# First dt transfers, sums and logarithms of the woven block moved ahead of the expert stage, and the last block's silus, convolutions and rows reordered

## What is computed

```
# first layer, attention place: a selective scan (8 groups of 128 inner features, 16 states)
hs, gate = in_proj(x)                      # 1024 + 1024
u   = silu(causal_conv4(hs) + cb)          # taps, then silu
ts, Bm, Cm = x_proj(u)                     # low rank 128, then 16 + 16 state rows
dt  = softplus(ts @ dt_proj + dt_b)
h_t = exp(dt_t * A) * h_(t-1) + (dt_t * u_t) * B_t
y   = (sum over states of h_t * C_t + D * u) * silu(gate);   out = y @ out_proj
# second layer: RWKV-like attention; a second selective scan on ctx (4 groups);
# a mixture of 8 experts (top 2 of a softmax router) and one shared expert: 33 tiles of 128 hidden features
out = sum_e C[t, e] * (silu(x @ Wg_e) * (x @ Wu_e)) @ Wd_e + sigmoid(x @ Wsg) * shared(x)
x = layernorm(x + out)
```

## Time and profile before

| | us |
|---|---|
| median of 3 runs (lowest, highest) | 4272.32 (4268.02, 4273.85) |
| profiled execution, its own time | 4263.87 |
| its span | 4262.0 |
| PE, DVE, ACT, POOL busy | 3528.0, 3220.0, 1624.2, 1278.1 |

### The profile page before, as it was taken

How to read it: one execution, slowest core, us unless ns; L and a number is a source line. 1 busy time by engine, 2 the same in 40 slices (tenths; PEclk the granted TensorE clock), 3 DMA queues, 4 the chain that set the end, 5 groups by cost and what they waited for, 6 DMA issues and landing times. The chain is left out here.

```text
span 4262.0 us, 40434 instructions
## 1 busy us (share of the span) xinstructions
PE 3528.0 (83%) x14823; PEld 1466.2 (34%) x14823; DVE 3220.0 (76%) x2759; ACT 1624.2 (38%) x2173; POOL 1278.1 (30%) x452
## 2 busy tenths in 40 slices
PE   5777759887899859887899859887899859875898
PEld 1222233333333333333333333333333333322443
DVE  5998469777899669778899668868899758866333
ACT  4766333124555233214655333213555343212101
POOL 1544204332344203342344303342244303332000
PEclk8888979989899979989899979989799979976999
DMA  4888402221233302122233302122233301110222
GB/s 156 306 324 315 160 15 82 70 82 65 89 99 102 126 16 74 67 81 75 81 99 102 133 16 74 67 77 79 72 103 104 121 32 67 67 60 15 87 92 77
DMA packets 91350, 418.52 MB, mean 98 GB/s; under 512 B 14224, under 2 KB 26640, under 8 KB 88720
## 3 DMA queue, kind: packets, MB, share of 16 engines
q1 hardware_dynamic: 69264, 384.44, 25.3%
q10 hardware_dynamic: 21888, 31.43, 2.8%
HBM read 320.45 MB, written 70.25 MB: 92 GB/s over the span
## 5 line engine op out<-in xcount | busy, mean ns | idle before, releaser
L276 PE MATMUL ps<-r,ring 128*128 128x512 bf16 (+2 forms) x2040 | 802.0, 394 | 0.0
L1105 POOL TENSOR_TENSOR hh<-hh,bc 128x2048 f32<-128x2048 f32 x72 | 337.8, 4692 | 1023.9 <-DVE hh L1028 1023.9
L273 PE MATMUL ps<-r,ring 128*128 128x512 bf16 (+2 forms) x1384 | 558.3, 404 | 95.1 <-POOL r L259 29.4
L273 PE MATMUL ps<-xr,ring 128*128 128x512 bf16 x1568 | 622.3, 397 | 12.7 <-DMA ring<-wsplit 12.7
L277 PE MATMUL ps<-xr,ring 128*128 128x512 bf16 x1568 | 619.4, 395 | 0.0
L277 PE MATMUL ps<-r,ring 128*128 128x512 bf16 (+2 forms) x1384 | 557.7, 404 | 0.0
L1105 POOL TENSOR_TENSOR bc<-bc 128x2048 f32<-128x2048 f32 x64 | 299.2, 4675 | 350.2 <-DVE bc L1028 350.2
L1105 POOL TENSOR_TENSOR r<-r,bc 128x2048 f32<-128x2048 f32 x56 | 262.7, 4691 | 314.3 <-DVE r L1028 314.3
L1028 DVE TENSOR_TENSOR_SCAN hh<-da,hh 128x2048 f32<-128x2048 f32 x72 | 328.0, 4555 | 13.0 <-ACT da L966 11.8
L1069 DVE TENSOR_TENSOR xc<-xc,ps 128x512 f32<-128x512 f32 x176 | 119.3, 678 | 249.5 <-PE ps L277 249.5
L1028 DVE TENSOR_TENSOR_SCAN bc<-da,bc 128x2048 f32<-128x2048 f32 x64 | 289.2, 4519 | 0.5
(11 more groups left out here) (244 smaller groups left out, 6507.3 us busy)
## 6 DMA issues: line engine op xcount, KB each, us to landing
ring<-wsplit SPq DMA_DIRECT2D x304, 768.0 KB, 4.2
r<-wstream SPq DMA_DIRECT2D x76, 768.0 KB, 7.4
wsplit<-ring SPq DMA_DIRECT2D x58, 768.0 KB, 4.7
da<-r ACTq DMA_DIRECT2D x384, 63.9 KB, 2.0
wsplit<-r SPq DMA_DIRECT2D x18, 768.0 KB, 6.1
r<-xT SPq DMA_DIRECT2D x7, 1024.0 KB, 5.5
r<-gates_dram SPq DMA_DIRECT2D x3, 2048.0 KB, 9.7
bc<-guwT SPq DMA_DIRECT2D x4, 1024.0 KB, 7.4
```

The costliest lines, as they stand in the source:

```text
L273: mm = pe.matmul(out, w_hi, x_hi, start=start, stop=False)
L276: pe.matmul(out, w_hi, x_lo, start=False, stop=False)
L1105: pool.tensor_tensor(quartet(s), quartet(s), k.out_rows, ALU.mult).then_inc(read, 1)
```

## The change

In `close_batch` the dt products get four banks and move ahead of the rows, ACT's and DVE's parts of them move with them, both logarithms stand where they were but fewer operations lie before and behind, only the first `total` stays, and the first dt*u group and the first two fetches of the expert stage are done here (one by SP, one by ACT, which also loads the exp table). In `hidden_and_scan` (expert stage) those are left out, the second half of the sum is done by DVE at step 1, and the early loads are issued by ACT at step 31 instead of by SP. In `second_preparation` (with a store) ACT takes all x copies, taps and the first silu before the norm's squares and the other silus before its factors; POOL makes three low halves of y0 before the first of the silus; three of the low-rank products move ahead of mix(3); the rows get four banks, and DVE copies the first four of them.

```diff
1077.84 1.40 DVE L368 ScanInputs: dt_bank(j) = self.dt_banks[j % len(self.dt_banks)], used by magnitude, positive and dt_product
-        if j >= 2:
-            pe.wait_ge(self.zread, j - 1)
+        if j >= len(self.dt_banks):
+            pe.wait_ge(self.zread, j - len(self.dt_banks) + 1)
1077.84 1.40 DVE L368 spread_row
-            if self.row_banks == self.banks:
-                pe.wait_ge(self.zread, self.J)
+        if r < count:
+            taken = [j + 1 for j in range(self.J) if self.dt_banks[j % len(self.dt_banks)] == self.row_banks[r]]
+            if taken:
+                pe.wait_ge(self.zread, taken[-1])
1077.84 1.40 DVE L368 second_preparation, tensor
+                for c in range(3):
+                    s.low_product(pe, c)
                 mix(3)
-            for c in range(J1):
+            for c in range(0 if here else 3, J1):
                 s.low_product(pe, c)
1077.84 1.40 DVE L368
                 mix(5)
+                pe.wait_ge(norm.out, 4)
1077.84 1.40 DVE L368 second_preparation, scalar
             copy_x(1)
             tap(1)
+            copy_x(2)
+            tap(2)
+            copy_x(3)
+            s.silu(act, 0)
+            tap(3)
             if norm:
                 norm.squares(act)
-            copy_x(2)
-            s.silu(act, 0)
-            tap(2)
-            copy_x(3)
             s.silu(act, 1)
-            tap(3)
+            s.silu(act, 2)
+            s.silu(act, 3)
             if norm:
                 norm.factors(act)
-            s.silu(act, 2)
-            s.silu(act, 3)
1077.84 1.40 DVE L368
-            for r in range(2 * GRP):
+            if not here:
+                act.wait_ge(s.row_in, GRP)
+            for r in range(0 if here else GRP, 2 * GRP):
                 s.act_row(act, r)
1077.84 1.40 DVE L368 second_preparation, gpsimd
-                mixer_low(0)
-                mixer_low(1)
+                for j in range(3):
+                    mixer_low(j)
                 s.split_x(pool, 0)
-                mixer_low(2)
                 s.split_x(pool, 1)
-                mixer_low(3)
                 s.split_x(pool, 2)
                 s.split_x(pool, 3)
+                mixer_low(3)
1077.84 1.40 DVE L368 second_preparation, vector
                 norm.sums(dve)
+                gate(2)
                 s.other_taps(dve, 0)
-                gate(2)
+                s.other_taps(dve, 1)
                 norm.centred(dve)
-                s.other_taps(dve, 1)
-                gate(3)
                 s.other_taps(dve, 2)
                 s.other_taps(dve, 3)
+                gate(3)
                 gate(4)
1077.84 1.40 DVE L368
+            if not here:
+                for r in range(GRP):
+                    s.dve_row(dve, r)
             for i in range(2):
                 s.total(dve, i)
1077.84 1.40 DVE L368 hidden_and_scan, sync: the early loads and the hold at slot + blocks - 2 are taken out
1077.84 1.40 DVE L368 hidden_and_scan, scalar
-                if s >= 2:
-                    act.wait_ge(scanned, s - 1)
+                if s == blocks // 2:
+                    act.wait_ge(late_sum, 1)
+                act.wait_ge(scanned, s - 1)
1077.84 1.40 DVE L368
-                    act.wait_ge(dt_in[s % 2], 64 * (s // 2 + 1))
+                    if s >= 2:
+                        act.wait_ge(dt_in[s % 2], 64 * (s // 2))
1077.84 1.40 DVE L368
-            if carried:
-                fetch(0)
-                fetch(1)
1077.84 1.40 DVE L368
+                if early and step == blocks - 1:
+                    act.wait_ge(dtx_mm, blocks)
+                    for dst, src in early:
+                        act.dma_start(dst, src).then_inc(early_in, 16)
1077.84 1.40 DVE L368 hidden_and_scan, vector
-            if which == 0:
+            if which == 0 and not made:
                 inputs_of(0)
1077.84 1.40 DVE L368
+                if carried and step == 1:
+                    half = slice(J // 2, J)
+                    dve.tensor_tensor(dt[:, half, :], dt[:, half, :], dtx[:, half, :], ALU.add).then_inc(late_sum, 1)
1077.84 1.40 DVE L368 close_batch: banks for dt (6, 7, 2, 3), for rows (4, 5, 6, 7)
+        def first_rows(engine, step):
+            for g in range(4):
+                engine.dma_start(k.da[step][32 * g:32 * g + 32, 0, 1:T], k.dt0[32 * step:32 * step + 32, 0, 1:T]).then_inc(first_in[step], 16)
1077.84 1.40 DVE L368 close_batch, sync
+                sp.wait_ge(s.dtsum, 1)
+                first_rows(sp, 0)
+                sp.wait_ge(first_in[0], 64)
1077.84 1.40 DVE L368 close_batch, tensor: low products 2 to 4 (was 2) between means and variances of the mixer's norm;
   dt products 0 to 3 | means | 4, 5 | variances | 6, 7 | rows | logits (was 0, 1 | means | 2, 3 | variances | rows | 4, 5 | logits | 6, 7)
1077.84 1.40 DVE L368 close_batch, scalar
             after_mixer.squares(act)
+            if ahead:
+                s.silu(act, J0 - 2)
             after_mixer.factors(act)
1077.84 1.40 DVE L368 magnitudes 0 to 3 | squares | 4, 5 | factors | 6, 7, exponential 0, 1 | router's tanh and exp | logarithm 0, 1 | weight rows, then
+                act.preload_act_table(ACT.Exp)
+                act.wait_ge(s.dtsum, 1)
+                first_rows(act, 1)
+                act.wait_ge(first_in[1], 64)
1077.84 1.40 DVE L368 close_batch, vector: positives 2 to 5 | rows 0 to 3 | scaled | positives 6, 7 | rows 4 to 7 | router, then
-                s.positive(dve, 6)
-                s.positive(dve, 7)
-            if ahead:
-                for i in range(2):
-                    s.total(dve, i)
+                s.total(dve, 0)
+                dve.wait_ge(s.dtsum, 1)
+                dve.tensor_tensor(k.dtx_now[:, 0, :], k.dt0[:, 0, :], k.y0[:, 0, :], ALU.mult)
```

More of the change, by code:

```diff
@@ L284, with __init__ @@
 class ScanInputs:
-    def __init__(self, k, which, source, banks, slots, row_banks=None):
+    def __init__(self, k, which, source, banks, slots, dt_banks=None, row_banks=None):
         self.k, self.which, self.source, self.banks, self.slots = k, which, source, banks, slots
+        self.dt_banks = dt_banks or banks
         self.row_banks = row_banks or banks
@@ L810, in hidden_and_scan @@
         carried = gated and blocks > 0
+        made = 1 if carried else 0
         def weight_bank(e):
@@ L827, in _ @@
         def _(sp):
-            if early:
-                k.w.load_until(sp, slot + blocks - 2, RING - 1, last)
-                for i in range(2):
-                    sp.wait_ge(dt_in[i], 64 * (blocks // 2))
-                sp.wait_ge(dtx_mm, blocks)
-                for dst, src in early:
-                    sp.dma_start(dst, src).then_inc(early_in, 16)
             stream_block(k, sp, slot + (hidden_slots(tiles) if tiles else 0), last)
-            if early:
-                sp.wait_ge(early_in, 16 * len(early))
             if splitter:
@@ L1010, in _ @@
                         splitter.high_part(act, n)
+            if early:
+                act.wait_ge(early_in, 16 * len(early))
         @blk.vector
@@ L1703, in close_batch @@
         mixed, turned, zg, yz = [sem(n) for n in ("mixed", "turned", "zg", "yz")]
+        first_in = [sem(f"first_in{i}") for i in range(2)]
         logits, st, ex, exd, sgd, gates, rows_mm = [
@@ L1708, in close_batch @@
         after_states = LayerNorm(k, "ln4", k.y1, k.xr, *stats)
-        s = ScanInputs(k, 0, lambda j: k.projected[:, j, :], (6, 7), {"low": W_PREP0, "dt": W_PREP0 + 1}, (2, 3, 4, 5)) if ahead else None
+        s = ScanInputs(k, 0, lambda j: k.projected[:, j, :], (6, 7), {"low": W_PREP0, "dt": W_PREP0 + 1}, (6, 7, 2, 3), (4, 5, 6, 7)) if ahead else None
         blk = ctx.enter_context(nc.Block())
@@ L1750, in _ @@
             if ahead:
-                s.low_product(pe, 2)
+                for j in range(2, 5):
+                    s.low_product(pe, j)
             after_mixer.variances(pe)
             if ahead:
-                for j in range(3, 7):
+                for j in range(5, 7):
                     s.low_product(pe, j)
@@ L1763, in _ @@
             if ahead:
-                s.dt_product(pe, 0)
-                s.dt_product(pe, 1)
+                for j in range(4):
+                    s.dt_product(pe, j)
             after_states.means(pe)
-            if ahead:
-                s.dt_product(pe, 2)
-                s.dt_product(pe, 3)
-            after_states.variances(pe)
-            if ahead:
-                for r in range(2 * GRP):
-                    s.spread_row(pe, r)
             if ahead:
@@ L1776, in _ @@
                 s.dt_product(pe, 5)
+            after_states.variances(pe)
+            if ahead:
+                s.dt_product(pe, 6)
+                s.dt_product(pe, 7)
+                for r in range(2 * GRP):
+                    s.spread_row(pe, r)
             for c in range(4):
@@ L1926, in _ @@
             if ahead:
-                s.positive(dve, 2)
-                s.positive(dve, 3)
+                for j in range(2, 6):
```

(1 more changed line is left out.)

45 lines of the change are left out of this document (22 added, 23 removed).

## The result

The changed kernel takes 4199.02 us (median; 4197.80 to 4205.07), the kernel before, run beside it, 4271.51 (4268.02 to 4273.85). The ratio is 0.9834, with the interval 0.9820 to 0.9849: faster by 1.7%. The forecast was 4201.8, in a range of 4188 to 4234. The profiled execution took 4199.06 us, its span is 4197.2.

The account below looks back on a forecast made before the run. PE bounds the steady expert stage (busy 40.00 of 40.00 us), waits between engines the last block. 14.4 (Parts 1, 2) + 15.9 + 40.2 = 70.5 us off 4263.87 gives 4193.4, plus 8.45 for the median 4201.8; range 4188 to 4234.

Parts of the forecast that it names:

- Part 1: Woven block's end: logits and totals finish earlier, 3.6 us gained in the first and third iteration, nothing in the second.
- Part 2: Expert stage's start: first scan 4.6 us earlier, less 2.25 for the late sum; with Part 1, 14.4 us in all.
- the prediction's sign: Expert stage's start: if right, the first scan comes about 4.5 us after the stage's first DVE operation.
- Rival A: Expert stage's start: lower PE clock or late decay, Part 2 gives nothing; 4216 us; shares 0.29 with two other rivals.
- Part 3: Expert stage's end: ring-slot waits (12.7 us) and two half-clock stretches (1.6 each) go; 15.9 us in all.
- Part 4: Last block: 8.6 us from the first gap and 4.8 from the rows, 13.4 per iteration, 40.2 in all.
- the first gap: Last block: PE's 6.04 us wait for POOL's third low half ahead of mix(2) goes; 8.6 us per iteration.
- Rival B: Last block gives only its first gap, 8.6 us per iteration; 4216 us; shares 0.29 with two other rivals.
- Rival E: Whole kernel: the change does nothing it says, other waits take over everywhere; 4272 us; chance 0.04.

Follow-up runs that it names:

- e12: Changed kernel with the woven block's old order and banks, the work moved across the border staying moved; 4213.63 us, ratio 0.9888.
- e3: Changed kernel with the first two groups of fetches, table load and first product back in the expert stage, new order kept; 4213.97 us, ratio 0.9859.
- e4: Changed kernel with the second half of the sum at step 1 put back in the woven block; 4201.89 us, ratio 0.9835.
- c1: The changed kernel run again with no edit; 4199.58 us, ratio 0.9823.
- e2: Changed kernel with the early loads back on SP behind the ring's loads, none issued by ACT; 4221.58 us, ratio 0.9874.
- e5: Changed kernel with only the last block's rows as before, four banks all copied by ACT; 4210.38 us, ratio 0.9856.
- e10: Changed kernel with ACT's old order of silus, copies and taps in the first preparation alone; 4201.46 us, ratio 0.9852.

## Why the prediction was right

Time and sign came out, 2.8 us from the forecast, and all four terms lie within 1.5 us of their sizes. That the total is so near is partly luck: the beginning alone moves by 14 us from one profile to the next, and the three ways of taking the difference give 64.7, 70.3 and 72.5 us. The terms don't all stand for what the prediction took them for.

**Part 1.** The steps hold, shifted by under 1 us: no wait for the logits; `total` 0 at 1080.17 - 4.0 = 1076.2 where I had 1075.6; SP's transfers done with ACT's. DVE's start was set by its own low halves, not by the logits' end as I had it. PE's first spread of the stage comes 62.7 us behind the woven block's sums in each iteration, where before it came after 66.6, 62.7 and 66.6: 3.9, 0.1 and 3.9 us gained for the 3.6, 0 and 3.6 predicted. That the second iteration gains less was right as well (W: -3.9 there, -7.8 in the others; predicted -4.6 and -8.2). The cause of the difference between the iterations, PE's clock up to and in the logits, fits e12, where all three run at the full clock and all three have the same W. The drain that the Trainium skill (ScalarE: Activation LUTs, What ACT_TABLE_LOAD costs) puts on top of each load doesn't show: the load at 1076.18 starts 0.02 us behind one activation and ends 0.01 before the next, and at the border ACT issued its last three transfers in 2.15 us beside the load of 1.28. The trace disagrees with the rule in these places.

**Part 2.** "Gain 4.6 us" was right as a place, too large by 0.75 us and wrong as a worth. The 9.1 us of before count from DVE's first operation (1088.25), the 4.5 of after from PE's first spread (1089.00 there, 1089.10 in after). From spread to scan it was 8.4, 8.3 and 8.3 us and is 4.5: 3.9 gained. Over three iterations that is 2.2 us, more than the 1.5 by which W falls short. From DVE's first operation, as the prediction's sign had it, the scan comes after 2.4 us, since the product that used to be this operation now lies in the woven block. Under the new order the stage's shorter start pays for the transfers at the woven block's end, and the move of everything across the border is worth 0.75 us (e3). Less the 2.25 us for the late sum, the move costs 1.5 us per iteration by these stretches; e3's longer time as a whole, most of it in the stretches named above, neither proves nor refutes this. The prediction had priced the landing of the transfers into part 1, so its sum was sound but for that 0.75, and it never compared the new order with the transfers left where they were. The late sum cost 2.2 to 2.3 us, as predicted (50.8 for 48.6 in the stretch of step 1), and it needn't have been moved (e4). Rival A, the start isn't carried, is out: X grew by no more than the sum, though clock steps of 1.6 us in both directions are in that figure (c1: 8.4 for 6.7).

**Part 3.** Right: no ring wait in any iteration, 16.5 us for 15.9; e2 brings 17.9 back. The split holds too: Y fell by 6.0, 3.8 and 6.8 us, the waits were 4.2, 3.6 and 4.9, and so 1.8, 0.2 and 1.9 are left for the half clock behind two of them, for the two times 1.6 of the prediction. The 6 us at or just behind each wait, in the kernel before:

```profile
1419.00:1425.00 6.00, 5.96 (x20) 2.34 (x21) 3.24 (x2) 0.60 (x1) 2.73 (x1) 0.72 0.50 177
2385.00:2391.00 6.00, 6.00 (x29) 2.59 (x27) 2.99 (x1) 0.60 (x1) 2.44 (x1) 1.00 0.36 135
3351.00:3357.00 6.00, 5.30 (x17) 2.04 (x18) 3.19 (x1) 0.60 (x1) 2.65 (x1) 0.72 0.43 159
```

The Trainium skill (DMA: Bandwidth & Descriptors, Issuing engines are not separate DMA queues) warns that issuing from another engine brings no bandwidth. The trace agrees in the main: the 2 MB took 8.7 us from ACT, 9.7 from SP and 9.4 from SP in e2. The gain was in when and in what order the transfers went out, not in bandwidth.

**Part 4.** Right, and by its own split: the rows 4.8 predicted and 4.9 measured per iteration (e5), the first gap 8.6 predicted and (41.6 - 14.8) / 3 = 8.9 left for it. The steps up to there came out to 0.4 us: in after, this block is 6.4 us earlier than in before; with that added the variances start at 1465.6 (1465.9 predicted), mix(3) at 1473.7 (1473.9) and mix(5) at 1488.3 (1488.7). POOL's halves were no wait for mix(3), as they were nearly none in the sum. What the prediction left on the table is the wait that stands at mix(5). The trace of after gives 4.1 us for it, where the earlier trace rows had 3.75, but it lacks the record of mix(5)'s first matmul, whose weights were loaded at 1481.96:

```profile
1481.96 0.10 PEld L273 LDWEIGHTS ps<-r,ring 128*128 128x128 bf16 x1 [4.22 <-issue]
```

So the wait is about 3.7 us, the same as before. I had carried mix(5) along as "keeps its order" and didn't ask what its wait was worth.

**Missed.** The new order on ACT acts in the first preparation too. By e10 it costs nothing that can be seen. The 4.2 us that the beginning grew by lie within what it does from one kernel's profile to the next. The other 1.6 us, right behind the last block, the prediction had at nothing: PE's clock differs there, though no edit lies there.

Rival B is out: the block gave 13.7 us on average. Rival E needs no word.

## What to carry over

When work is moved across a border between blocks, compare with the version in which only the order changes: a transfer that is taken from the head of one block can become the tail of the one before, and each half alone had most of the gain here (15.0 and 17.2 of 19.5 us). Of the waits that remain in the profile after a change, take the one whose releaser has an idle engine in front of it; the cheapest step of this case (three gates moved into a gap, 10.8 us) was in a wait that the prediction had listed and left. Cut two profiles at operations that both have and compare the pieces: most repeat to 0.1 us where totals move by 10, and those that don't (1.6 to 3.7 us) show where the clock changed.

## What the runs showed of the hardware

A stretch in which PE is busy for 10.00 of 10.00 us can still lose its clock (granted 0.83, 1.6 us), where a small saving some 190 us earlier was the only edit. Such steps of about 1.6 us appear and go in stretches with the same instructions, between kernels and between executions of one.

Thirty-two small matmuls (128x9) took 3.63 us at the full clock and 6.1 or 6.83 at the lower, in the same place of the program. In the kernel before, the stretch of half clock that holds them made the first and the third iteration 4.0 us longer there than the second.

The beginning of the program took 547.8 to 562.2 us over the ten profiled executions that have the same instructions there, and 549.7 to 560.5 over the four with ACT's old order.

In e3 and e12 PE was granted 0.50 instead of 1.00 for the first 6 us behind the last block of the third iteration, with the edit two stages earlier, and the stretch there took 3.7 us longer.
